# The state input's factor as a logarithm in the exponents: a Mamba-style block on one core

## The reference

```
tc = cumsum(theta);  B, C = rope(B, tc), rope(C, tc)          # per head
alpha = exp(dt*A);  gamma = lam*dt;  beta = (1-lam)*dt*alpha
h_t = alpha_t*h_{t-1} + gamma_t * x_t B_t + beta_t * x_{t-1} B_{t-1}
y_t = h_t C_t + D*x_t
out = u + (rms(y * silu(z)) @ out_proj.T) * silu(fp8_quantised_linear(layernorm(u)))
```

## Time and profile before

| | |
|---|---|
| median of 3 runs | 1283.85 us (1281.26 to 1285.37) |
| profiled execution, its own time | 1283.93 us |
| its span, first to last instruction | 1282.2 us |
| prologue, up to the first rotation of the main part | 138.8 us |
| main part | about 1143 us, 64 steps |
| busy over the span | PE 1124.5 (88%), DVE 1195.0 (93%), ACT 737.9 (58%), POOL 736.5 (57%) |

### The profile page before, as it was taken

The page is one execution under the profiler, slowest core; times in us unless marked ns, Lnnn a source line. Parts: engine busy times, 40 slices in busy tenths (PEclk is TensorE's granted clock), DMA queues, the critical chain, the costliest instruction groups (busy, mean ns, idle before and its releaser), DMA issues. The chain is left out here.

```text
span 1282.2 us, 30215 instructions
## 1 busy us (share of the span) xinstructions
PE 1124.5 (88%) x11410; PEld 819.9 (64%) x11410; DVE 1195.0 (93%) x1925; ACT 737.9 (58%) x1133; POOL 736.5 (57%) x588
## 2 busy tenths in 40 slices
PE   3876499998999999999999899989999899999996
PEld 3752366766666666666666666666667666666665
DVE  7998599998999899998999899999999899989994
ACT  4776155555655565556655655556555656556553
POOL 4000166666666666565766576657666576666664
PEclk9876699999999999999999999999999999999998
DMA  8534464345544355445544454346444455434441
GB/s 187 185 99 123 111 139 102 97 93 123 126 117 97 74 146 113 100 104 108 112 107 103 114 130 102 88 96 150 108 109 91 107 122 117 100 88 90 106 98 26
DMA packets 88468, 141.26 MB, mean 110 GB/s; under 512 B 16099, under 2 KB 35268, under 8 KB 88004
## 3 DMA queue, kind: packets, MB, share of 16 engines
q1 hardware_dynamic: 88323, 139.33, 46.4%
HBM read 57.89 MB, written 12.58 MB: 55 GB/s over the span
## 5 line engine op out<-in xcount | busy, mean ns | idle before, releaser
L1412 POOL TENSOR_TENSOR rot<-part 128x512 f32<-128x512 f32 x256 | 375.5, 1468 | 507.7 <-DVE part L1220 507.1
L1220 DVE SCALAR_TENSOR_TENSOR part<-bcs,k_prmT,k_trig 128x512 f32<-128x512 f32 x512 | 502.0, 1028 | 22.1 <-DMA bcs<-bc_t 12.4
L1353 ACT ACTIVATE E<-d 128x512 f32<-128x512 f32 x256 | 151.8, 593 | 192.5 <-PE d L1051 192.5
L1062 PE MATMUL s<-rot 64*128 64x128 f32 x2048 | 150.4, 286 | 26.6 <-POOL rot L1412 26.3
L1388 ACT ACTIVATE sz<-r 128x512 f32<-128x512 f32 x128 | 76.5, 597 | 165.5 <-PE r L1137 165.4
L1062 PEld LDWEIGHTS s<-rot 64*128 64x128 f32 x2048 | 127.6, 189 | 64.6 <-issue 64.4
L1238 DVE TENSOR_TENSOR M<-s,E 128x512 f32<-128x512 f32 x256 | 163.7, 679 | 2.4 <-PE s L1062 1.8
L1421 POOL TENSOR_TENSOR ce<-rot,eb 128x512 f32<-128x512 f32 x128 | 160.1, 1271 | 0.0
L1465 POOL TENSOR_TENSOR sqa<-sqa,sq 128x512 f32<-128x512 f32 x112 | 142.5, 1272 | 16.2 <-ACT sq L1358 7.8
L1036 PE MATMUL r<-k_w_zx,xns 128*128 128x256 f32 x512 | 131.8, 383 | 12.5 <-DMA xns<-xn_t 12.5
L1149 PE MATMUL y<-M,xk 128*64 128x128 f32 x2048 | 140.1, 279 | 0.0
(11 more groups left out here) (243 smaller groups left out, 1671.1 us busy)
## 6 DMA issues: line engine op xcount, KB each, us to landing
k_trig<-k_tri SPq DMA_DIRECT2D x512, 128.0 KB, 2.4
eb<-ecum_rows SPq DMA_DIRECT2D x128, 256.0 KB, 4.7
bcs<-bc_t SPq DMA_DIRECT2D x16, 256.0 KB, 3.9
bcs<-bc_t SPq DMA_DIRECT2D x32, 128.0 KB, 3.9
a_big<-in_L_attn_u SPq DMA_DIRECT2D x4, 512.0 KB, 6.3
xn_t<-a_xnT SPq DMA_DIRECT2D x1, 2048.0 KB, 10.7
tc_t<-a_tcT SPq DMA_DIRECT2D x1, 2048.0 KB, 15.9
bc_t<-a_tmp SPq DMA_DIRECT2D x1, 2048.0 KB, 8.5
```

Source lines behind the costliest of these rows:

```text
L1062: last = nc.tensor.matmul(Sp[j][:, k], rot[rows, q % 2, p, 0, k], rot[rows, q % 2, p, 1, k], start=True, stop=True)
L1220: nc.vector.scalar_tensor_tensor(out=part[:, 2 * p + f, :], in0=bcs[:, (t + q // NQ) % 2, 2 * w + f, :], scalar=col, in1=trig[:, p, 1 - f, ...
L1353: nc.scalar.activation(E[:, h % 2, :], Dp[:], ACT.Exp).then_inc(e_ready, 1)
L1412: nc.gpsimd.tensor_tensor(rot[:, q % 2, p, w, :], part[:, 2 * p, :], part[:, 2 * p + 1, :], ALU.add).then_inc(rot_ready, 1)
```

## The change

1. `kk` is no longer multiplied into x. In the prologue, log K is computed (clamped at zero, plus 2^-100), cut into three bf16 parts like the cumulative logs, transposed, copied and stored in `log_parts`; 12 more rows of `pick` hold it and 12 more rows of `cum` hold ones, so the exponent matmul has 123 rows instead of 111. `dec` is multiplied by K once, by GpSimd.
2. In a step ScalarE copies x from R[0] and R[1] to `xk` (`x_copy`). VectorE makes only `xc`, after the copy of the same bank, and M for heads 2 and 3 stands between the two.
3. The projection of group 7 and the sum of squares move into the next super's first step (`project(t, -1)`, `square_sums`, now in bank Yp[0]); the norm's start, root, reciprocal, refinement and `normalised` move later by up to a step.

```diff
@@ prepare, sync
+                if t == 5:
+                    sp.wait_ge(logT_out, 4)
+                    for i in range(3):
+                        sp.dma_start(logs_d.rearrange("t c i h s -> i h (t c) s")[i],
+                                     cumT[H * i:H * i + H, :].rearrange("h (x s) -> h x s", s=P)).then_inc(logs_stored, 16)
@@ prepare, gpsimd
+            for i in range(2):
+                pool.wait_ge(log_cut, i + 1)
+                nc.gpsimd.tensor_tensor(s[2].rearrange("p (c h) -> p c h", h=H), s[2].rearrange("p (c h) -> p c h", h=H), cum3[:, :, H * i:H * i + H], ALU.subtract).then_inc(log_left, 1)
+            pool.wait_ge(dec_done, 1)
+            nc.gpsimd.tensor_tensor(K["dec"][:], K["dec"][:], kk[:], ALU.mult).then_inc(log_left, 1)
@@ prepare, tensor, in the gate loop
+                if t in (3, 4):
+                    pe.wait_ge(log_cut, 3)
+                    for g in (2 * t - 6, 2 * t - 5):
...
+                        for i in range(8):
+                            last = nc.tensor.transpose(ps_bf[g % 2][0:3 * H, i, :], cum3[:, 8 * g + i, :], K["ident_bf"][:])
+                        last.then_inc(logT_t, 1)
@@ prepare, scalar
             for g in (0, 2):
+                if g == 2:
+                    act.wait_ge(kk_done, 2)
+                    nc.scalar.activation(s[2], kk[:], ACT.Ln).then_inc(log_left, 1)
...
+            def log_part(i):
+                act.wait_ge(log_left, i + 1)
+                act.wait_ge(cumT_t, 4)
+                nc.scalar.copy(cum3[:, :, H * i:H * i + H], s[2].rearrange("p (c h) -> p c h", h=H)).then_inc(log_cut, 1)
+
+            log_part(0)
             for t in range(NS):
                 if t + 2 < NS:
                     gate_input(t + 2)
+                if t in (1, 3):
+                    log_part((t + 1) // 2)
...
+                if t in (3, 4):
+                    act.wait_ge(cum_stored, 64)
+                    for g in (2 * t - 6, 2 * t - 5):
+                        act.wait_ge(logT_t, g + 1)
+                        nc.scalar.copy(cumT[:, 1024 * g:1024 * g + 1024],
+                                       ps_bf[g % 2][0:3 * H].rearrange("p c t -> p (c t)")).then_inc(logT_out, 1)
@@ units, tensor
+            def square_sums(t):
+
+                pe.wait_ge(yt_ready, at(T2, t, T2))
+                pe.wait_ge(sqa_ready, at(T2, t, T2))
+                for c in range(CS):
+                    last = nc.tensor.matmul(Yp[0][:, c:c + 1], sqa[:, c * P:c * P + P], K["ones"][:, 0:1],
+                                            start=True, stop=True)
+                last.then_inc(ssq_ready, 1)
...
                     exponents(t, q, 3)
+                    if q == 0 and t > 0:
+                        square_sums(t - 1)
...
-                    if q > 0:
+                    if t + q > 0 and q != 1:
                         project(t, q - 1, (0, 1))
                     pe.wait_ge(hch, at(T8, t, 8 * q + 8))
                     if live(t, q + 1):
                         x_by_token(t, q + 1, 1)
-                    if q > 0:
-                        project(t, q - 1, (2, 3))
+                    if t + q > 0:
+                        project(t, q - 1, (2, 3) if q != 1 else range(CS))
...
+                    if q == 0:
+                        pe.wait_ge(ssq_taken, at(1, t, 0))
@@ units, vector
             def x_scaled(t, q, tt, i):
-                dve.wait_ge(x_ready, at(T2, t, 2 * q + i + 1))
+                dve.wait_ge(x_copied, at(T2, t, 2 * q + i + 1))
...
-                    if q == 0 and t > 0:
-                        norm_start(t - 1)
                     if live(t, q + 2):
                         angles(t, q + 2)
                     for c in range(CS):
                         state(t, q, c)
                     if live(t, q + 1):
                         rotation(t, q + 1, 0, 0, 1)
                         x_scaled(t, q + 1, tn, 0)
-                        x_scaled(t, q + 1, tn, 1)
                     scores(t, q, 2)
                     scores(t, q, 3)
                     if q == 0 and t > 0:
-                        norm_seeded(t - 1)
+                        norm_start(t - 1)
+                    if live(t, q + 1):
+                        x_scaled(t, q + 1, tn, 1)
@@ units, scalar
+            def x_copy(t, q, i):
+                act.wait_ge(x_ready, at(T2, t, 2 * q + i + 1))
+                act.wait_ge(y_ready, at(T2, t, 2 * q - 2))
+                nc.scalar.copy(xk[:, q % 2, 2 * i:2 * i + 2, :].rearrange("p c k -> p (c k)"), R[i][:]).then_inc(x_copied, 1)
...
                     decays(t, q, 2)
                     decays(t, q, 3)
+                    if q == 1 and t > 0:
+                        normalised(t - 1)
+                    if live(t, q + 1):
+                        x_copy(t, q + 1, 0)
+                        x_copy(t, q + 1, 1)
                     if q == 0 and t > 0:
                         root(t - 1)
```

More of the change, by code:

```diff
@@ L49 @@
 OWN_S = OWN_T + 3
-D_ROWS = OWN_S + 3 * CS
+OWN_L = OWN_S + 3 * CS
+D_ROWS = OWN_L + 3 * CS
 FAR = 2.0 ** 100
@@ L217, in _ @@
             fill(cum[MASK_ROWS:OWN_T], own[MASK_ROWS:OWN_T, :], 8)
-            fill(cum[OWN_S:D_ROWS], own[OWN_S:D_ROWS, :], 8)
+            fill(cum[OWN_S:OWN_L], own[OWN_S:OWN_L, :], 8)
+            fill(cum[OWN_L:D_ROWS], own_log[OWN_L:D_ROWS, :], 8)
             by_super = lambda a: a[:].rearrange("p (s t) -> p s t", s=NS)
@@ L310, in _ @@
             link(nc.gpsimd.memset(own[OWN_T:OWN_S, :], 1.0))
-            pool.sem_inc(masks, 1)
+            mine = own_log[OWN_T:D_ROWS, :].rearrange("r (c s) -> r c s", c=CS)
+            link(nc.gpsimd.memset(own_log[OWN_T:D_ROWS, :], 1.0))
+            for base, mult in ((-3 - 3 * CS, 1), (5 + 3 * CS, -1)):
+                link(nc.gpsimd.affine_select(out=mine, in_=mine, compare_op=ALU.is_ge, fill=0.0, base=base,
+                                             pattern=[[-3 * mult, CS], [0, P]], channel_multiplier=mult))
+            pool.sem_inc(masks, 1)
+            for i in range(2):
[3 more added lines that the diff above has]
+            nc.gpsimd.tensor_tensor(K["dec"][:], K["dec"][:], kk[:], ALU.mult).then_inc(log_left, 1)
         weights = [[stage2[:, 0:P], stage2[0:2 * H, 9 * P:10 * P]]]
@@ L642, in _ @@
                 a, b = 512 * i, 512 * i + 512
-                by4 = lambda x: x.rearrange("p (g k) -> p g k", k=4)
                 dve.wait_ge(shift_t, i + 1)
-                for dst, head in PLACES:
-                    link(nc.vector.tensor_tensor(by4(K["kk"][:, a:b])[:, :, dst], by4(gam[:, a:b])[:, :, head],
-                                                 by4(ps[i][:])[:, :, head], ALU.add))
+                link(nc.vector.tensor_tensor(kk[:, a:b], gam[:, a:b], ps[i][:], ALU.add))
+                nc.vector.tensor_scalar(kk[:, a:b], kk[:, a:b], 0.0, TINY, ALU.max, ALU.add).then_inc(kk_done, 1)
                 link(nc.vector.tensor_tensor(s[3][:, a:b], s[3][:, a:b], ps[i][:], ALU.mult))
@@ L1067, in project @@
             def project(t, q, chunks):
+                t, q = (t, q) if q >= 0 else (t - 1, NQ - 1)
                 if q == 0 and chunks[0] == 0:
@@ L1174, in _ @@
                     exponents(t, q + 1, 1)
-                project(t, NQ - 1, range(CS))
-                pe.wait_ge(sqa_ready, at(T2, t, T2))
-                pe.wait_ge(e_ready, at(T4, t, T4 + 2 if live(t, NQ) else T4))
-                for c in range(CS):
-                    last = nc.tensor.matmul(Dp[:, c:c + 1], sqa[:, c * P:c * P + P], K["ones"][:, 0:1],
-                                            start=True, stop=True)
-                last.then_inc(ssq_ready, 1)
+            project(NS - 1, NQ - 1, range(CS))
+            square_sums(NS - 1)
         @block.vector
@@ L1304, in _ @@
                             rotation(t, q + 1, p, w, 1)
+                            if q == 0 and t > 0 and (p, w) == (1, 0):
+                                norm_seeded(t - 1)
                     for p in range(2):
@@ L1331, in _ @@
             act.sem_inc(absd, 3)
-            for s in (e_ready, sz_ready, sq_ready, acc_done):
+            for s in (e_ready, x_copied, sz_ready, sq_ready, acc_done):
                 act.sem_inc(s, 1)
@@ L1396, in _ @@
                     squares(t, q, 1)
-                    if q == 0 and t > 0:
-                        normalised(t - 1)
             root(NS - 1)
@@ L1450, in _ @@
                     c_decayed(t, q)
-                    if q == 0 and t > 0:
-                        norm_refined(t - 1)
                     if live(t, q + 1):
@@ L1485, in program @@
         cum_stored = ctx.enter_context(nc.semaphore("cum_stored"))
-        prepare(nc, K, dram, scratch, cum_stored)
-        units(nc, K, dram[0], scratch, cum_stored, out)
+        logs_stored = ctx.enter_context(nc.semaphore("logs_stored"))
+        prepare(nc, K, dram, scratch, cum_stored, logs_stored)
+        units(nc, K, dram[0], scratch, cum_stored, logs_stored, out)
```

62 lines of the change are left out of this document (38 added, 24 removed).

## The result

The kernel after takes 1261.01 us (1259.11 to 1261.22, 4 runs) against 1282.77 us (1281.26 to 1285.37, 4 runs) of the kernel before: ratio 0.9825, 95% interval [0.9805, 0.9845]. It is faster by 22 us where 79 were forecast, and slower than the upper end of the range, 1236.

A forecast was written before the change was run, and what follows sets the result against it. VectorE was taken to set the step, TensorE right behind; 1283.93 - 76.8 (`xk`) - 23.9 + 11.2 (turns) + 6.4 (balance) + 4.7 (prologue) - 0.6 (main part's head) = 1204.9, stated as 1205 us, range 1194 to 1236.

The forecast's parts named there:

- The bound: Main part's step: VectorE sets it at 17.02 us, with TensorE right behind at 15.87 us of work.
- the balance term: Main part: small delays between nearly level VectorE and TensorE, 0.1 us in each of 64 steps, +6.4 us.
- The xk term: VectorE's steps: 128 `xk` writes removed at 0.60 us each, -76.8 us; step from 17.02 to 15.82 us.
- Rival B: VectorE's rotations: one more slowed beside GpSimd each step, 64 by 0.31 us, giving 1225 us; chance 0.17 with E's TensorE limit.
- Its sign: VectorE's lone rotations in the main part would all read 1.06 us or more.
- Rival C: VectorE's rotations: one meeting GpSimd waits for its whole instruction, 1.27 us a step, 81 us back, 1286 us; chance 0.02.
- The turn: Between supers: VectorE's waits of 3.42 us go, 7 times, -23.9 us; late additions of 1.6 us each, +11.2 us.
- The prologue: Before the main part: added ScalarE and TensorE work delays the last Silu and the start of loads, +4.7 us.
- A: Main part: ScalarE's copies are late in every step, 0.5 us a step, 32 us, giving 1237 us; chance 0.14.
- Rival D: Main part: the loop through ScalarE closes, exposing both copies, 1.6 us a step, 102 us, giving 1307 us; chance 0.04.
- The 123 rows: Exponent matmul: 123 rows instead of 111 priced at nothing, since the columns are the same.

The follow-up runs named there:

- e1: Kernel after, with GpSimd's two `ce` products moved ahead of the first sum of rotated parts in each step; 1226.18 us, ratio to before 0.9587.
- e5: Kernel after, with GpSimd's `ce` products cut from 512 to 4 columns after the first step; 1222.91 us, ratio to before 0.9549.
- e7: Kernel before with only the change's third part (projection, sum of squares and norm moved later); 1269.91 us, ratio 0.9904.
- e6: Kernel after, prologue only: two subtractions moved from GpSimd to VectorE, `dec` times K later, third cut earlier; 1260.24 us, ratio to before 0.9808.
- e3: Kernel after without ScalarE's copies of x from the third step on, `xc` waiting for TensorE directly; 1257.2 us, ratio to before 0.98.

## Why the prediction was wrong

**The bound** was right: VectorE sets the step, and TensorE with 15.87 us is next. The balance of the two was charged with 0.1 us a step (bounds 0 and 0.25), and where `ce` is out of the way (e1, e5) a plain step stays 0.3 to 0.4 us above 15.87, at 16.12 to 16.31. By e5's rows that is in the main the first rotation of the step behind the sums of squares (1.48 instead of 1.06), for which the angles and then TensorE's x matmuls wait. The kernel after never gets so far, so this is not in its miss; it is why e1 and not the forecast shows what the change could give.

**The xk term** is the step that failed: "VectorE's step becomes 17.02 - 1.20 = 15.82 us here". It took the writes as plain work. They were also the cover under which GpSimd's `ce` ran, since they read PSUM. I priced the pull-forward of the rotations as a gain for `rot` (its wait of 0.39) and did not ask what GpSimd would be doing at that moment. The answer stands in GpSimd's timeline of before, of which the prediction has no row for `ce` and which I did not set beside VectorE's: `ce` ends at 637.39, the rotations begin at 637.08; there was no slack at all. Measured: -76.8 became -14 with the rotations' +63.1.

**Rival B** named the right event (one more rotation beside GpSimd in each step) at 0.31 us, from the one row of 1.06; that is why it gave 1225. Its sign, lone rotations at 1.06 or more, looked at the wrong ones: the lone rotations read 1.07 and 0.74 in a step of the kernel after, as before, and the new long one is among the six. **Rival C** had the right mechanism (a rotation waits for the whole instruction) and nearly the price, 1.27 us where it was 1.0, and got 0.02. With the measured terms in the forecast's sum, 1204.9 + 63.1 (rotations) - 6.4 (the balance term, as TensorE still waits) + 6.1 (prologue) - 4.7 (turns, both below) = 1263.0; the profiled run took 1261.08. The terms overlap a little at the turns, so the 2 us between them say nothing. The reading that ruled C out was wrong: 1.06 is 0.75 plus the rest of GpSimd's instruction. By the trace GpSimd's sums of squares end at 627.61 + 2.69 = 630.30 there, and 629.78 + 1.06 - 0.75 = 630.09, the same 0.2 us before the end as above. And the six rotations of the earlier trace rows, 6.22 us, cannot be six of 0.66 and the like: two long ones of 1.76 are in them. The section of the Trainium skill that the prediction set aside for this row was right, and this row agrees with it.

**The turn**: -23.9 for the waits and +11.2 for the additions. The waits went; the additions were 0.66 and 0.57 instead of 0.8 each; e7, which has no copies, gives -12.5. In the kernel after the turns' periods give -17.4, and the first of the two waits costs less than its length, since a VectorE that comes later to its rotations meets less of `ce` (in that step they are 1.89 + 4.75 us and not 7.19).

**The prologue**: +4.7 forecast for the last Silu and with it for the main part; +9.0 came at the Silu and +10.8 at the first rotation, so 1.8 us more come behind it, which the prediction had at nothing: SyncE issues the main part's first load 5.6 us after the last Silu starts (141.64) where it was 3.3 (130.40). No run says why. The three stopped quantising operations are 5.8 us. I had counted GpSimd's subtractions at 2.5 to 3 us for TensorE's wait, and never put them beside VectorE's two-input operations. With them away 4.9 us are left (e6), near the 4.7, but with other work in them.

**The copies** (A): not late in plain steps, 8.3 us of waits in all, e3 gives 4 us. Rival D did not happen. The 123 rows cost nothing (group L1102: 389 ns, 390 before).

## What to carry to other kernels

When an edit takes work off VectorE, ask which of its instructions slide against GpSimd's. In these traces the instructions that read PSUM are free cover for GpSimd (M stays at 0.69 us or less), while a rotation, with its inputs in SBUF, and a GpSimd instruction exclude each other, and the later one pays the rest of the earlier (1.76 against 0.74, 1.72 against 1.28). So read GpSimd's timeline next to VectorE's even if GpSimd is 40% idle, and move its work away from the two-input instructions first: here 35 us for swapping two lines. A duration a little over the usual one (1.06 for 0.75) is no evidence of sharing; check whether the excess ends with the other engine's instruction.
